# Full 128-column slices for routed transposes, and a broadcast product moved from VectorE to GpSimd

## What is computed

```python
x = x + 0.5 * L0_ffn(layernorm(x))   # 16 experts, 4 per token, width 176, and a shared expert of width 704
x = x + L0_attn(layernorm(x))        # 16 heads of 16, l2-normed q, k, v, causal
x = x + 0.5 * L0_ffn(layernorm(x))
x = x + 0.5 * L1_ffn(layernorm(x))   # 32 experts, at most 8 per token, width 96
x = x + L1_attn(layernorm(x))        # gated state-space block, width 512, 8 heads
x = x + 0.5 * L1_ffn(layernorm(x))
# an expert: h = silu(x @ w_gate.T) * (x @ w_up.T); acc += (h @ w_down.T) * combine_weight[:, None]
```

## Time and profile before

| | before |
|---|---|
| median of 3 runs | 989.24 us (989.04 to 990.76) |
| profiled execution, its own time | 989.24 us |
| its span, first to last instruction | 987.4 us |
| mean granted TensorE clock | 0.974 of full speed |

### The profile page before, as it was taken

How to read it: one execution, slowest core, us unless ns; L and a number is a source line. 1 busy time by engine, 2 the same in 40 slices (tenths; PEclk the granted TensorE clock), 3 DMA queues, 4 the chain that set the end, 5 groups by cost and what they waited for, 6 DMA issues and landing times.

```text
span 987.4 us, 20904 instructions
## 1 busy us (share of the span) xinstructions
PE 888.0 (90%) x6996; PEld 550.9 (56%) x6996; DVE 701.0 (71%) x1392; ACT 493.4 (50%) x865; POOL 480.5 (49%) x465
## 2 busy tenths in 40 slices
PE   2768889999938899899999989899999999999997
PEld 1355556666624666657665545454566445666564
DVE  6786524786789987735644898887879788875554
ACT  2856543577824577544755773344433553333322
POOL 3766267513586435277742888532433224422322
PEclk9978999999959999999999999999999999999999
DMA  9688545633121232957793542111110211112222
GB/s 304 258 220 173 122 132 124 130 77 81 61 75 64 76 72 72 223 199 138 174 191 117 159 142 85 59 52 54 43 54 23 78 50 48 54 45 87 71 69 64
DMA packets 123268, 106.63 MB, mean 108 GB/s; under 512 B 75672, under 2 KB 97944, under 8 KB 123168
## 3 DMA queue, kind: packets, MB, share of 16 engines
q1 hardware_dynamic: 117024, 88.51, 32.9%
q0 software_dynamic: 6144, 16.79, 5.9%
HBM read 58.98 MB, written 30.02 MB: 90 GB/s over the span
## 4 chain that ended last, share of the span: by engine, by line
PE 36%; DVE 5%; POOL 5%; issue 3%; ACT 1%; DMA 0%; POOLq 0%; DVEq 0%; SPq 0%; ACTq 0%
PE ps L1062 18%; PE ps L1111 9%; POOL wlo L771 2%; PE ps L1093 2%; PE ps L1037 2%; POOL hh L717 1%; POOL back L760 1%; PE ps L1255 1%; PE ps L1286 1%; PE ps L1275 1%; DVE hid L1329 1%; DVE scr L1660 1%; PE ps L1265 1%; PE ps L1079 1%; DVE hid L1337 1%
## 5 line engine op out<-in xcount | busy, mean ns | idle before, releaser
L717 POOL TENSOR_TENSOR hh<-hid,hh 128x512 f16<-128x512 f32 x120 | 144.6, 1205 | 256.0 <-ACT hh L828 255.6
L1323 DVE SCALAR_TENSOR_TENSOR hid<-gtanh,ps 128x512 f32<-128x512 f32 (+2 forms) x184 | 114.3, 621 | 153.2 <-ACT gtanh L808 150.6
L1062 PE MATMUL ps<-xhi,whi 128*128 128x512 f16 x480 | 184.5, 384 | 22.7 <-DVE hid L1323 18.5
L808 ACT ACTIVATE gtanh<-ps 128x512 f32<-128x512 f32 (+2 forms) x184 | 100.5, 546 | 193.5 <-PE ps L1062 158.3
L1062 PE MATMUL ps<-xlo,whi 128*128 128x512 f16 x480 | 184.2, 384 | 0.0
L1062 PE MATMUL ps<-xhi,wlo 128*128 128x512 f16 x480 | 184.0, 383 | 0.0
L1111 PE MATMUL ps<-whi,hh 128*128 128x256 f16 x960 | 176.3, 274 | 2.0 <-POOL hh L717 1.5
L1337 DVE SCALAR_TENSOR_TENSOR hid<-hid,ps 128x512 f32<-128x512 f32 (+2 forms) x184 | 114.4, 621 | 54.6 <-PE ps L1037 27.7
L1037 PE MATMUL ps<-whi,xs_sb 128*128 x992 | 127.9, 243 | 20.2 <-issue 13.5
L1111 PE MATMUL ps<-wlo,hh 128*128 128x256 f16 x480 | 131.4, 274 | 0.0
L828 ACT ACTIVATE hh<-hid 128x512 f16<-128x512 f32 x120 | 75.2, 627 | 110.1 <-DVE hid L1329 82.9
(11 more groups left out here) (208 smaller groups left out, 1579.5 us busy)
## 6 DMA issues: line engine op xcount, KB each, us to landing
ys_dram<-y_sb SPq DMA_DIRECT2D x60, 256.0 KB
xs_sb<-c_dram SPq DMA_DIRECT2D x64, 192.0 KB, 2.8
scr<-w_in SPq DMA_DIRECT2D x28, 384.0 KB, 4.3
scr<-we_in SPq DMA_DIRECT2D x32, 304.0 KB, 4.2
xs_sb<-c_dram SPq DMA_DIRECT2D x64, 128.0 KB, 3.0
xs_sb<-c_dram SPq DMA_DIRECT2D x64, 64.0 KB, 2.7
xs_dram<-y_sb SPq DMA_DIRECT2D x1, 3968.0 KB, 15.0
scr<-ws_in SPq DMA_DIRECT2D x8, 384.0 KB, 6.9
```

Of the source, the lines that this page charges most:

```text
L717: pool.tensor_tensor(hlo[:, k, :], hid[:, k % 2, :], hhi[:, k, :], ALU.subtract).then_inc(lo_done, 1)
L808: act.activation(gtanh[:, n % 2, 0:w], ps[:, G_BANK, 0:w], ACT.Tanh, scale=0.5 / W_SCALE)\
L1062: mm = pe.matmul(ps[:, bank, :], w[:, off:off + P], a[:, kc, t0:t0 + HN], start=(i == 0), stop=(i == 3 * KC - 1))
L1323: dve.scalar_tensor_tensor(out=hid[:, k, 0:w], in0=gtanh[:, k, 0:w], scalar=1.0, in1=ps[:, G_BANK, 0:w], op0=ALU.add, op1=ALU.mult).then_i ...
```

## The change

The first part sets IA to 128 and IB to 48 and adds a third piece to `hp`: the last 48 columns of hi stand again behind lo. A block is then turned with three transposes of 128 columns each, at columns 0 (hi), 176 (lo) and 272 (the last 80 of lo and the 48 of the copy); the weights in `down` are laid out to fit, with 32 zero rows. All five matmuls of `down` have 128 rows. ACT gets one more small copy for each routed unit. The second part moves `fac` from DVE to POOL. The whole `ORDER` table is written anew for it. `ones8` becomes a view of `onesf` (one memset less at the start).

```diff
-IA = 112
+IA = P
...
         if kind == F1:
             put("SP", "f", "load_fac", u)
-            put("DVE", "m", "fac", u)
+            put("POOL", "f", "fac", u)
...
-        hp = sb("hp", [P, 2, 2, 2, I0], F16)
+        hp = sb("hp", [P, 2, 2, 2 * I0 + IB], F16)
...
+                if name == "fac":
+                    m = n - UNIT[F1_PASSES[0]]
+                    pool.wait_ge(h_ready, n + 1)
+                    pool.wait_ge(fac_loaded[m % FRING], 32 * (m // FRING + 1))
+                    pool.tensor_tensor(hid[:, n % 2, :], hid[:, n % 2, :], fac[:, m % FRING, :], ALU.mult).then_inc(fac_done, 1)
...
+                        h = hid[:, n % 2, 0:w * I0].rearrange("p (b i) -> p b i", i=I0)
+                        act.activation(hp[:, m % 2, 0:w, 0:I0], h, ACT.Copy).then_inc(hi_done, 1)
+                        act.activation(hp[:, m % 2, 0:w, 2 * I0:2 * I0 + IB], h[:, :, IA:I0], ACT.Copy).then_inc(tail_done, 1)
...
                     pe.wait_ge(lo_done, n + 1)
+                    pe.wait_ge(tail_done, m + 1)
...
-                        for out, part in ((hT[:, at:at + P], hp[:, m % 2, b, 0, 0:P]),
-                                          (hT[:, at + P:at + 2 * P], hp[:, m % 2, b, 1, 0:P]),
-                                          (hT[0:IB, at + 2 * P:at + 3 * P], hp[:, m % 2, b, 0, IA:I0]),
-                                          (hT[IB:P, at + 2 * P:at + 3 * P], hp[:, m % 2, b, 1, IA:I0])):
-                            mm = pe.transpose(out, part, ident16[:, :])
+                        for i, col in enumerate((0, I0, 2 * I0 + IB - P)):
+                            mm = pe.transpose(hT[:, at + P * i:at + P * i + P], hp[:, m % 2, b, col:col + P], ident16[:, :])
...
-                                                                 (2, whi, P, D), (2, wlo, IB, D))):
+                                                                 (2, whi, P, D), (2, wlo, P, D))):
...
-                elif name == "fac":
-                    m = n - UNIT[F1_PASSES[0]]
-                    dve.wait_ge(h_ready, n + 1)
-                    dve.wait_ge(fac_loaded[m % FRING], 32 * (m // FRING + 1))
-                    dve.tensor_tensor(hid[:, n % 2, :], hid[:, n % 2, :], fac[:, m % FRING, :], ALU.mult).then_inc(fac_done, 1)
```

More of the change, by code:

```diff
@@ L376, in build @@
         inactive = sb("inactive", [P, HT, 8])
-        ones8 = sb("ones8", [P, 8])
+        ones8 = onesf[:, 0:8]
         esum = sb("esum", [P, HT])
@@ L491, in build @@
         turned, hT_done, y_out = sem("turned"), sem("hT_done"), sem("y_out")
+        tail_done = sem("tail_done")
         y_stored = [sem(f"y_stored{k}") for k in range(YRING)]
@@ L625, in piece @@
                 elif name == "blank":
-                    sp_.wait_ge(pool_consts, 5)
+                    sp_.wait_ge(pool_consts, 4)
                     sp_.dma_start(xs_dram.rearrange("(b p) c -> p b c", p=P),
@@ L702, in _ @@
             pool.memset(onesf[:, :], 1.0).then_inc(pool_consts, 1)
-            pool.memset(ones8[:, :], 1.0).then_inc(pool_consts, 1)
-            pool.wait_ge(pool_consts, 5)
+            pool.wait_ge(pool_consts, 4)
             def piece(name, n):
-                if name == "lo":
+                if name == "fac":
[3 more added lines that the diff above has]
+                    pool.tensor_tensor(hid[:, n % 2, :], hid[:, n % 2, :], fac[:, m % FRING, :], ALU.mult).then_inc(fac_done, 1)
+                elif name == "lo":
                     k = n % 4
@@ L713, in piece @@
                         j, w = (BLOCK[r] + c) % 2, xs_loads(c)
-                        pool.tensor_tensor(hp[:, j, 0:w, 1, 0:I0], hid[:, n % 2, 0:w * I0].rearrange("p (b i) -> p b i", i=I0),
-                                           hp[:, j, 0:w, 0, 0:I0], ALU.subtract).then_inc(lo_done, 1)
+                        pool.tensor_tensor(hp[:, j, 0:w, I0:2 * I0], hid[:, n % 2, 0:w * I0].rearrange("p (b i) -> p b i", i=I0),
+                                           hp[:, j, 0:w, 0:I0], ALU.subtract).then_inc(lo_done, 1)
                     else:
@@ L817, in piece @@
                             act.wait_ge(turned, m - 1)
-                        act.activation(hp[:, m % 2, 0:w, 0, 0:I0], hid[:, n % 2, 0:w * I0].rearrange("p (b i) -> p b i", i=I0),
-                                       ACT.Copy).then_inc(hi_done, 1)
+                        h = hid[:, n % 2, 0:w * I0].rearrange("p (b i) -> p b i", i=I0)
+                        act.activation(hp[:, m % 2, 0:w, 0:I0], h, ACT.Copy).then_inc(hi_done, 1)
+                        act.activation(hp[:, m % 2, 0:w, 2 * I0:2 * I0 + IB], h[:, :, IA:I0], ACT.Copy).then_inc(tail_done, 1)
                     else:
@@ L1000, in _ @@
             pe.wait_ge(act_consts, 2)
-            pe.wait_ge(pool_consts, 5)
+            pe.wait_ge(pool_consts, 4)
             at_expert = [pe.alloc_register(f"at_expert{k}") for k in range(2 * REGS)]
@@ L1321, in piece @@
                         dve.wait_ge(lo_done, n - 1)
+                        r2, c2 = WHERE[n - 2]
+                        if PASSES[r2][0] == RT:
+                            dve.wait_ge(tail_done, BLOCK[r2] + c2 + 1)
                     dve.scalar_tensor_tensor(out=hid[:, k, 0:w], in0=gtanh[:, k, 0:w], scalar=1.0, in1=ps[:, G_BANK, 0:w],
                                              op0=ALU.add, op1=ALU.mult).then_inc(act_done, 1)
-                elif name == "fac":
-                    m = n - UNIT[F1_PASSES[0]]
-                    dve.wait_ge(h_ready, n + 1)
-                    dve.wait_ge(fac_loaded[m % FRING], 32 * (m // FRING + 1))
-                    dve.tensor_tensor(hid[:, n % 2, :], hid[:, n % 2, :], fac[:, m % FRING, :], ALU.mult).then_inc(fac_done, 1)
                 elif name == "h":
@@ L1390, in piece @@
                     e = E0 if n < 4 else E1
-                    dve.wait_ge(pool_consts, 5)
+                    dve.wait_ge(pool_consts, 4)
                     dve.wait_ge(logits_ready, n + 1)
@@ L1750, in lay_out @@
     dn = dn.transpose(0, 2, 1)
-    we[:, 0:IA, 2 * KC * I0:2 * KC * I0 + D] = dn[:, 0:IA]
-    for at in (0, IB):
+    we[:, :, 2 * KC * I0:2 * KC * I0 + D] = dn[:, 0:IA]
+    for at in (P - IB, P - 2 * IB):
         we[:, at:at + IB, 2 * KC * I0 + D:] = dn[:, IA:]
```

## The result

The change made the kernel faster by 3 us where 29 were forecast: 985.43 us in the median of 20 runs against 988.80, ratio 0.9967 (95% interval 0.9954 to 0.9979). A second set gave 0.9951 (0.9933 to 0.9969). The time lies outside the range of 940 to 980. The profiled execution took 984.44 us, its span 982.6.

What follows compares the result with a forecast made beforehand. PE's matmul stream was taken to bound the kernel nearly everywhere; 989.2 - 36 (slices) + 13 (`fac` in dense 3/0) - 2 (other dense passes) - 4 (rewritten order) = 960 us, range 940 to 980.

Steps and rivals of the forecast that it cites:

- The rewritten order ... I take -4: First pass: PE's 10.06 us wait behind three held DVE operations shrinks, as POOL's run gets shorter by one piece; -4 us.
- I take +13: Dense pass 3/0: 22 added `fac` fill POOL, window at least 106 us instead of 96.7, plus waits; +13 us.
- not over 95%: Sign expected in dense 3/0 behind the last routed unit: POOL busy over 95%, that part longer by some 13 us.
- The slices, -36: Routed stretches: full tiles and fewer transposes shorten PE's stream; 36 us of the 52 removed arrive.
- 52 us to be removed from PE's stream: Routed units: 0.42 us less PE work a block in `down` and `turn`, over 124 blocks.
- 8, 9, 8 and 11 forecast: Microseconds by which the four routed stretches, in order, were to get shorter, of 13 removed in each.
- -2 was forecast: Dense passes other than 3/0: `fac` on POOL fits beside PE's units and the last chain hides; -2 us.
- DVE and POOL take over: Rival, chance 0.19: attention stretches give 4 each, the others 8 and 10, dense 3/0 costs 20; 979 us.
- The slices don't do it: Rival, chance 0.04: `down`'s 0.10 us steps come from address registers, not tile shape; slices win only 7; 989 us.
- POOL starves DVE: Rival, chance 0.05: beside the state-space block, DVE instructions wait for POOL, costing 23 us in each of two passes; 1006 us.

Runs made afterwards that it cites:

- groups 2 and 4: Two of five groups of follow-up runs, each group on a chip of its own; the kernel before has its median at 988 to 990 us in both.

## Why the prediction was wrong

It summed 989.2 - 36 + 13 - 2 - 4 = 960. Worked out from the ratios of groups 2 and 4 times 988: slices -24 (0.9758), order and `fac` together +19 (0.9951 less 0.9758), together -5. The forecast had +7 for order and `fac` together (13 - 2 - 4), so each of the two halves missed by 12 us.

**The step that failed: adding the order and `fac` as terms of their own, "The rewritten order ... I take -4" and "I take +13".** They don't add. Put the order first and it costs +17 (0.9932 less 0.9758), and `fac` in it 0 to +2. Put `fac` first, in the order of before for which it was worked out, and it costs +25 where 11 were forecast, and the new order then gives 6 back, near the -4. What both have in common is 3/0: 112.8 us with neither, 123.7 with the order, 134.7 with `fac` and 126.3 with both (groups 2 and 4). PE waits there for a `lo` or an `act` that stands behind a bunch of other items on POOL or DVE. I bounded POOL by its total: 102.7 us of busy time from the first blocked piece to unit 111's `lo`, and a window of 106 to 110. The busy time came out, 103.2, but the window is 119.8 us; POOL is busy for 86% of it, not over 95%. The sum of a queue was the wrong bound; the wait of one unit behind what is bunched ahead of it sets it.

I priced the order from one place, the three DVE operations held for 11 us. That stall stayed: a DVE operation at 49.94 us takes 8.01 us, and PE waits 4.55 us at 53 instead of 10.06, but the first pass got 0.9 us longer. What the new order does elsewhere I hadn't priced: -8.6 in 0/1 and -4 in 3/1, but +11 in 3/0, +6.6 in 2/0, +7.5 in the shared passes of the third stage and +1.6 in the last pass (traces of the new order with `fac` on DVE, group 2, against the slices alone, group 4). Why 2/0 and the shared passes got longer stays open. The `ORDER` table of the changed kernel has the bunches in 3/0 (`c2 w f w c l` on POOL), and I read it as "nothing has left POOL's list". How many items stand ahead of each `lo` was the question.

**The slices, -36: mechanism right, size off by 12.** The matmuls go at 0.108, the transposes as taken, the copy on ACT at 0.273 us (0.28 taken) beside `lo`. Of the 52 us to be removed from PE's stream, 37 are gone from its busy time, 8 to 10 in each routed stage. Of 8, 9, 8 and 11 forecast, 4.7, 3.3, 6.3 and 2.7 arrived in the old order. For 2/1, with the most forecast, I weighed only the work of DVE and ACT, and left out the register loads on PE's own queue: idle time put down to "issue" is 3.2 us before and 9.0 with the slices, and at the place shown the `gate` starts right behind the two loads, before and after. But the loads are not where the missing 12 us went. With constant offsets the slices still bring only 3.9 us in 2/1 and 18 in the four stretches. Loads and address operations are a cost beside the slices, 27 us in the kernel before and 22 with the slices by the ratios. What holds the rest of the slices' gain stays open; the waits of PE in 2/1 that are left are for DVE, ACT and DMAs of token blocks.

**`fac` on POOL, +13 in 3/0: right in place, near the number by chance.** 3/0 got longer by 14.9, of which `fac` has some 2.5 on top of the new order; in the order for which it was worked out it costs 22. A `fac` takes 1.27 us, not 1.158. For the other three passes -2 was forecast: 3/1 and 5/0 gave 4.7, and the last pass took 1.6 back, so that no last chain was hidden. 3/1's part is the order's (122.8 us with `fac` on DVE too), 5/0's goes with `fac` (122.9 on DVE, 121.6 on POOL), the last pass's is the order's (101.7 with either).

**The rivals.** "DVE and POOL take over" (979) was nearest: POOL's +20 in 3/0 is what `fac` costs in the old order, and the two attention stretches gave 3.3 and 6.3 with the slices alone, near its 4 each. But PE's long wait for DVE there, 11.9 us in 0/1, was there before with 11.1. "The slices don't do it" (989) is near in time, and its mechanism fell: full tiles took the steps away, with the address registers as they were. "POOL starves DVE" beside the state-space block fell: those passes got no longer, though single DVE operations there did, one product of two tiles from 0.69 to 1.64 us. (Its figures 1.158 and 0.691 bear on the price alone, not on the port; and only one of its two passes has 118 such instructions, the other 100.) None of the rivals was the order.

## What to carry to other kernels

A rewritten static order and an operation moved within it are one term, not two: here the same move cost 25 us in the old order and at most 2 in the new one, which cost 17 by itself. Price both by how many items stand ahead of each piece that another engine waits for, not by a queue's total; a part of an order, transplanted, need not keep its stage lengths. And before idle time put down to "issue" is blamed for a missing gain, take its cause out of the old kernel as well as of the new one: here the gain missing from the slices was missing without the loads too.

## What the runs showed of the hardware

A register load on PE's queue takes 0.30 us, 0.44 from one to the next, and PE's matmuls stop behind two of them, for 0.87 us at the place shown. Without 92 of the 124 loads the kernel was 17 us faster. The product of two f32 tiles takes POOL 1.27 us where the `lo` of the same size takes 1.158 with one f16 operand. A DVE product of two tiles, 0.69 us by itself, took 3.87 while POOL ran two pieces in a row. Behind 5.46 us without a matmul PE's matmuls started 0.43 us apart instead of 0.22 for some 4 us, at a granted clock of 0.50. The same kernel had medians of 988 to 990 and 999 to 1000 us on different chips, at granted clocks of about 0.975 and 0.969.
